# A two-layer graph kernel: the edge stage sums two blocks into the same banks, ten blocks' raw rows go ahead instead of seven, and the second aggregation gathers seven units a block

## What is computed

```python
h = relu(layernorm(x))
h1 = relu(sage_conv(h, src, dst, W1l, W1r, b1))      # mean over in-edges of h[src] @ Wl.T, + b + h @ Wr.T
x = x + sage_conv(h1, src, dst, W2l, W2r, b2)
h = relu(layernorm(x))
e = relu(concat([h[src], h[dst], edge_attr]) @ W1 + b1)
x = x + segment_mean(e @ W2 + b2, src)               # mean over the edges of each src
```

## Time and profile before

| what | us |
|---|---|
| median of 3 runs | 6354.2 (6326.7 to 6368.4) |
| the profiled execution | 6340.2 |
| its span | 6338.4 |
| PE busy | 4354.8 (69%) |
| DVE busy | 3739.4 (59%) |
| POOL busy | 2891.2 (46%) |
| ACT busy | 2546.9 (40%) |

### The profile page before, as it was taken

The page is one execution under the profiler, slowest core; times in us unless marked ns, Lnnn a source line. Parts: engine busy times, 40 slices in busy tenths (PEclk is TensorE's granted clock), DMA queues, the critical chain, the costliest instruction groups (busy, mean ns, idle before and its releaser), DMA issues. The chain is left out here.

```text
span 6338.4 us, 173060 instructions
## 1 busy us (share of the span) xinstructions
PE 4354.8 (69%) x64842; PEld 3895.0 (61%) x64842; DVE 3739.4 (59%) x6428; ACT 2546.9 (40%) x5151; POOL 2891.2 (46%) x2761
## 2 busy tenths in 40 slices
PE   3889888885777777743666666666666656666656
PEld 3778777774767666643655556556556555555656
DVE  7888888885655556553544554544544544545456
ACT  2445445443444444422433333333333333333334
POOL 2666656654554545454333443443433443444341
PEclk8999999997999989975777777777777777777778
DMA  4533233333444433323342333333333333334332
GB/s 87 124 92 76 71 74 75 74 74 95 113 113 108 107 80 85 81 56 103 97 106 89 100 103 98 99 101 99 100 93 101 103 97 107 97 94 111 92 97 60
DMA packets 509079, 591.17 MB, mean 93 GB/s; under 512 B 203666, under 2 KB 462721, under 8 KB 508278
## 3 DMA queue, kind: packets, MB, share of 16 engines
q1 hardware_dynamic: 423190, 479.51, 28.5%
q0 software_dynamic: 84032, 103.47, 6.9%
q10 hardware_dynamic: 1266, 0.31, 0.0%
HBM read 481.80 MB, written 101.17 MB: 92 GB/s over the span
## 5 line engine op out<-in xcount | busy, mean ns | idle before, releaser
L1603 POOL DMA_INDIRECT sorted_edges<-edge_rows,edge_index x1356 | 1321.7, 975 | 2015.9 <-ACT edge_rows L1725 1554.6
L1110 POOL DMA_INDIRECT conv_got<-parts_table,conv_index x1060 | 1235.4, 1165 | 876.8 <-PE conv_sums L1156 336.6
L1225 ACT CAST conv_rows<-conv_rows_ps 128x384 bf16<-128x384 f32 x2226 | 999.3, 459 | 1283.1 <-PE conv_rows_ps L1139 1040.0
L1139 PE MATMUL conv_rows_ps<-parts,conv_hot_t 128*128 128x192 bf16 x8268 | 1111.2, 256 | 451.7 <-ACT conv_rows L1225 237.0
L1689 PE MATMUL edge_sums<-edge_parts,edge_hot 128*128 128x64 bf16 (+1 forms) x15582 | 792.9, 209 | 565.5 <-issue 516.5
L1674 PE MATMUL edge_a_ps<-parts,edge_hot_t 128*128 128x64 bf16 x15582 | 792.9, 213 | 469.6 <-issue 466.2
L1156 PE MATMUL conv_sums<-conv_rows,conv_hot_d 128*128 128x193 bf16 (+1 forms) x8268 | 1103.4, 255 | 0.5 <-issue 0.4
L1689 PEld LDWEIGHTS edge_sums<-edge_parts,edge_hot 128*128 128x128 bf16 x15582 | 674.8, 108 | 668.7 <-issue 607.9
L1139 PEld LDWEIGHTS conv_rows_ps<-parts,conv_hot_t 128*128 128x128 bf16 x8268 | 698.4, 101 | 587.3 <-ACT conv_rows L1225 286.5
L1674 PEld LDWEIGHTS edge_a_ps<-parts,edge_hot_t 128*128 128x128 bf16 x15582 | 678.6, 111 | 560.8 <-issue 558.5
L1740 ACT ACTIVATE edge_parts<-edge_a_ps 128x448 bf16<-128x448 f32 x371 | 204.9, 552 | 1850.3 <-DVE edge_a_ps L1863 1413.5
(11 more groups left out here) (208 smaller groups left out, 5161.0 us busy)
## 6 DMA issues: line engine op xcount, KB each, us to landing
edge_slot_row<-slot_rows SPq DMA_DIRECT2D x371, 224.0 KB
conv_slot_row<-slot_rows SPq DMA_DIRECT2D x424, 192.0 KB
edge_edges<-sorted_edges SPq DMA_DIRECT2D x322, 224.0 KB
conv_slot_row<-slot_rows SPq DMA_DIRECT2D x318, 160.0 KB
edge_dst_row<-dst_rows SPq DMA_DIRECT2D x226, 192.0 KB
edge_attr<-in_edge_attr SPq DMA_DIRECT2D x225, 192.0 KB
sorted_edges<-edge_rows,edge_index POOLq DMA_INDIRECT x1356
sorted_edges<-conv_zero SPq DMA_DIRECT2D x28, 632.0 KB
```

The source lines that it names most:

```text
L1110: pool.indirect_dma_start(got[g][:, f, 0:PARTS * D], None, k.parts_table, bass.IndirectOffsetOnAxis(ap=index[h][:, g, at:at + 1], axis=0)) ...
L1139: mm = pe.matmul(rows_ps[(bs * h + i) % banks][:, at:at + PARTS * D], hot_t[home[g]][:, v, u * P:(u + 1) * P], k.parts[:, 2 * (GU * g + u) ...
L1225: act.copy(rows[i % bufs][:, 0:n, 0:PARTS * D], rows_ps[(bs * h + i) % banks][:, 0:n * PARTS * D].rearrange("p (u d) -> p u d", u=n)).then ...
L1603: pool.indirect_dma_start(k.sorted, bass.IndirectOffsetOnAxis(ap=index[s.part.ring][0:used, at:at + 1], axis=0), rows[j][0:used, t, :], No ...
```

## The change

Three things. (1) Ten blocks are early instead of seven. A round has six items, five of them ordinary, and there are eight rounds behind one early item and ahead of four. The ring in HBM holds five blocks, early chunks ahead of the edge stage are 46, and POOL sends four scatters a block in the second aggregation; SP loads the chunks as fast. (2) In a round the items go in pairs, and groups alternate: group g of one block, then group g of the other, then g+1. PE sums both into the same banks without a start in between (`opens`, `closes`), and DVE adds them once. Buffers turn by the place in the order (`r`), no longer by g. 25 parts are spread over the 42 slots of a round. The first round is written out, the other seven are a loop. (3) In the second aggregation one unit of each group is gathered, seven a block, and the others are expanded.

```diff
-EARLY, ROUND, ROUNDS, AHEAD, STARTED, EARLY_AT = 7, 7, 6, 3, 4, 2
+EARLY, ROUND, ROUNDS, STARTED = 10, 5, 8, 3
+LONG = (ROUND + 1) * NG
-EARLY_BUFS, BETWEEN, AFTER = 4, 5, 3
+EARLY_BUFS, BETWEEN, AFTER, EACH = 4, 5, 3, 4
...
-        fetched = [1 + g % 2 for g in range(NG)]
+        fetched = [1 + g % 2 if sorting else 1 for g in range(NG)]
...
-                    if b % 3 == 0:
-                        k.early.load(sp, BETWEEN + EARLY_BUFS + (b // 3 - 2))
+                    if b >= 3:
+                        k.early.load(sp, BETWEEN + 2 + EACH * b // ET)
...
-                    k.early.scatter(pool, 2)
+                    k.early.scatter(pool, EACH)
...
-                    pe.wait_ge(got_landed[g], 16 * fetched[g] * (done + b + 1))
+                    pe.wait_ge(got_landed[g], 16 * fetched[g] * (b + 1) + 16 * (1 + g % 2) * done)
...
         def round_group(i, s):
-            w, g = s // NG, s % NG
-            item, parity = AHEAD + (ROUND + 1) * i + w, (AHEAD + w) % 2
-            if w == EARLY_AT:
-                return Group(item, g, True, i + 1, parity, None)
-            n = AHEAD - 1 + w - (1 if w > EARLY_AT else 0)
-            return Group(item, g, False, ROUND * i + n, parity, n % RB)
+            d, s = s // LONG, s % LONG
+            pair_no, at = s // (2 * NG), s % (2 * NG)
+            g, side = at // 2, at % 2
+            early = pair_no == 1 and side == 0
+            n = (side, 2, 3 + side)[pair_no]
+            before = (at + 1, 2 * NG + g + 1, 3 * NG + at + 1)[pair_no]
+            index = i + (d + 1) if early else ROUND * i + (ROUND * d + n)
+            done = NG * i + (NG * (d + 1) + g + 1) if early else ROUND * NG * i + (ROUND * NG * d + before)
+            return Group(LONG * i + (LONG * d + s + NG), LONG // NG * i + (LONG // NG * d + s // NG + 2), s % NG, g, early, index, done,
+                         6 * i + (6 * d + 2 * pair_no + side + 1), 3 * NG * i + (3 * NG * d + NG * (pair_no + 1) + g), n, side == 0, side == 1)
 
         def round_part(i, p):
-            n, j = p // ES, p % ES
-            w = n - (AHEAD - 1)
-            read = AHEAD + (ROUND + 1) * i + w + (1 if w >= EARLY_AT else 0)
-            return Part(ROUND * i + (n + STARTED), j, (n + STARTED) % RB, read)
+            d, m, j = p // (ROUND * ES), p // ES % ROUND, p % ES
+            return Part(ROUND * i + (ROUND * d + STARTED + m), j, (STARTED + m) % RB, 6 * i + (6 * d + (1, 1, 3, 3, 5)[m]))
...
-                wait_alone(act, third_made, group.number + 1)
+                wait_alone(act, third_made, group.number + NG)
...
-                        dve.wait_ge(scattered[s], 16 * ET * Part(b - 3, s, None).times)
+                        dve.wait_ge(scattered[s], 16 * ET * Part(b - 2, s, None).times)
...
             def sum_up(group):
-                    if w % GU == 0:
-                        pe.wait_ge(added, 2 * group.number + half + 2)
+                    if w % GU == 0 and group.opens:
+                        pe.wait_ge(added, 2 * group.tally + half + 2)
...
-                        mm = pe.matmul(to[:, 0:n], hot[at][:, u, v * P:(v + 1) * P], parts[at][:, u, i, 0:n], start=(i == 0), stop=(i == PARTS - 1), skip_group_check=True)
+                        mm = pe.matmul(to[:, 0:n], hot[at][:, u, v * P:(v + 1) * P], parts[at][:, u, i, 0:n], start=(group.opens and w % GU == 0 and i == 0),
+                                       stop=(group.closes and w % GU == GU - 1 and i == PARTS - 1), skip_group_check=True)
...
-                if s.two_back is not None:
+                if s.two_back is not None and s.two_back.closes:
                     add_sums(s.two_back)
```

More of the change, by code:

```diff
@@ L1376, with __init__ @@
 class Group:
-    def __init__(self, item, g, early, index, parity, ring):
-        self.item, self.g, self.early, self.index, self.parity, self.ring = item, g, early, index, parity, ring
-        self.number = NG * item + g
-        self.done = NG * index + g + 1
+    def __init__(self, number, turn, r, g, early, index, done, item, tally, ring, opens, closes):
+        self.number, self.turn, self.r, self.g = number, turn, r, g
+        self.early, self.index, self.done, self.ring = early, index, done, ring
+        self.item, self.tally, self.opens, self.closes = item, tally, opens, closes
+        self.parity = 1 if closes else 0
 class Part:
@@ L1533, in take @@
             def take(group, before):
-                g, item = group.g, group.item
+                g, r = group.g, group.r
+                made = group.number + 1
+                if not isinstance(made, int):
+                    made = sp.to_reg(made)
                 if g == 0 and not group.early:
@@ L1540, in take @@
                         wait_positive(sp, scattered[s], both[min(s, 1)])
-                if g == 0 and group.early and not isinstance(item, int):
+                if g == 0 and group.early and not (isinstance(group.index, int) and group.index == 0):
                     for j in range(1, ES):
                         k.early.wait_chunk(sp, EARLY * ES - ES + j)
-                    sp.wait_ge(expanded, NG * (item - 3) + 2 * NG)
-                sp.wait_ge(hot_t_made, group.number + 1)
-                sp.wait_ge(other_made, group.number + 1)
-                sp.dma_start(slot_row[g][:], k.slot_rows[bass.ds(block_of(group), 1), g * GU * P:(g + 1) * GU * P].to_broadcast([P, GU * P])).then_inc(row_landed[g], 16)
-                if before is None and g >= NG - 2:
+                    sp.wait_ge(expanded, group.number + 1 - 2 * NG + NG)
+                sp.wait_ge(hot_t_made, made)
+                sp.wait_ge(other_made, made)
+                sp.dma_start(slot_row[r][:], k.slot_rows[bass.ds(block_of(group), 1), g * GU * P:(g + 1) * GU * P].to_broadcast([P, GU * P])).then_inc(row_landed[r], 16)
+                if before is None and r >= NG - 2:
                     sp.wait_ge(split, 2 * GROUPS)
@@ L1595, in slot @@
                     if s.part.read is not None:
-                        for g in range(NG):
-                            pool.wait_ge(edges_landed[g], 16 * (s.part.read + 1))
+                        for landed in edges_landed:
+                            pool.wait_ge(landed, 16 * s.part.read)
                 wait_alone(pool, rows_ready, s.part.q + 1)
@@ L1640, in early_turn @@
             def early_turn(group, part):
-                pe.wait_ge(edges_landed[group.g], 16 * (group.item + 1))
+                pe.wait_ge(edges_landed[group.r], 16 * group.turn)
                 pe.wait_ge(attr_ready, part.q + 1)
@@ L1678, in sum_up @@
             def sum_up(group):
-                at = home[group.g]
+                at = home[group.r]
                 pe.wait_ge(third_made, group.number + 1 + NG + 1)
@@ L1843, in make_hot_t @@
             def make_hot_t(group):
-                g, at = group.g, home[group.g]
-                dve.wait_ge(row_landed[g], 16 * (group.item + 1))
-                dve.wait_ge(expanded, group.number + 1 - since[g] + NG)
-                dve.tensor_scalar(hot_t[at][:, 0, :], slot_row[g][:], k.node_of[:, 0:1], None, ALU.is_equal).then_inc(hot_t_made, 1)
+                g, at = group.g, home[group.r]
+                dve.wait_ge(row_landed[group.r], 16 * group.turn)
+                dve.wait_ge(expanded, group.number + 1 - since[group.r] + NG)
+                dve.tensor_scalar(hot_t[at][:, 0, :], slot_row[group.r][:], k.node_of[:, 0:1], None, ALU.is_equal).then_inc(hot_t_made, 1)
             def make_early_hot(group):
@@ L1887, in add_sums @@
                     dve.wait_ge(summed, 2 * (group.number + NG) + half + 1)
-                    dve.wait_ge(added, 2 * group.number + half + 2)
+                    dve.wait_ge(added, 2 * group.tally + half + 2)
                     dve.tensor_tensor(part, part, sums[half][:, 0:GU * D1].rearrange("p (w d) -> p w d", d=D1), ALU.add).then_inc(added, 1)
```

85 lines of the change are left out of this document (42 added, 43 removed).

## The result

On the same chip, in turns with the kernel before, the changed kernel takes 6107.6 us (median of four, 6089.8 to 6110.1) and the kernel before 6344.8 us (6326.7 to 6368.4): a ratio of **0.962, interval 0.959 to 0.965**, 237 us less. Forecast were 6262 us, with a range from 6140. The sign is right; the size is 2.8 times the forecast's 85 us, and the time lies under the range.

A forecast was written before the change was run, and what follows sets the result against it. Runs of indirect scatters were taken to stop PE in the edge stage. Terms -89 - 21 - 13 + 35 + 3 = -85 took 6340.2 to 6255 us; 6262 was named, between that and 6269, range 6140 to 6370.

The forecast's parts named there:

- The second aggregation, +35 forecast: Second aggregation: two more scatters and three fewer gathers a block, with added matmuls, cost +0.78 us a block, +35 us in all.
- the gather's price of 0.6 us: Second aggregation: each gather taken away saves 0.6 us, chosen between 0.50 and 0.71.
- The bound of -9 for this stage: Second aggregation, lower bound: every POOL DMA at one price, 0.59 us, gives -0.09 us a block, -9 in all.
- P at a = 4.39: Edge stage: P, a part's PE work and six scatters, put at 7.22 us if an ordinary group (a) takes 4.39.
- Parts and early blocks -89: Edge stage: 15 fewer parts (90 scatters) and 21 groups turned early save 89 us, the middle of -68 and -110.
- adds -21: Edge stage: pairing two blocks relieves 182 groups of DVE's adds, saving 21 us, bounds 0 and -195.
- Projection ahead -13 forecast: Projection ahead of the edge stage: POOL sends 28 early scatters instead of 38, saving 13 us, bounds 0 and -16.
- First aggregation +3 forecast: First aggregation: three more early blocks are cleared at 1.1 us each, costing 3 us.
- Rival 1, VectorE's turn decides: Edge stage body: DVE's turn bounds it, so saved adds count: 6102 us in full, 6200 at half; chance 0.20.
- Rival 2, the toll only moves: Scatters cost the same in aggregation and edge stage, gathers were cheap, adds hidden: 6337 us, no change; chance 0.22.
- Rival 3, slower by runs of scatters: Second aggregation: four scatters make a run of five, removed gathers cost nothing: +153 us there, 6415 in all; chance 0.11.
- Rival 4: The change doesn't do what it says: paired order costs a wait each round or parts bunch; 6290 to 6300 us.

## Why the prediction was wrong, point by point

- **The second aggregation, +35 forecast, -114 found, is the step that failed, and in it the gather's price of 0.6 us.** It came from dividing ten gathers' 5.0 us by ten or by seven, as if each cost alike. By runs: three gathers fewer a block, and nothing else, gave 1208.2 - 979.6 = 229 us, 1.4 us for each of the 159, though six matmuls a block were added; by the one block without scatters the seven that remain cost 1.3 us in all. What has a price is the place in a run, and not the gather: without the second gathers the runs are shorter, and 122 DMAs fewer stand third or later. The trace before had shown the stop in a run of scatters. The prediction used it for its slower rival alone, and not for gathers taken away. It also read it as "every further one", where the second still leaves PE 23 matmuls in 1.28 us and only from the third on it stands nearly still.
- The scatter's price was right: 1.04 us forecast. Seven gathers alone against the change, the same but for two scatters more in fifty blocks (and a little else), are 979.6 and 1093.7: 1.14 us each, though across two sets of runs.
- The bound of -9 for this stage was no bound. It spread the difference of two kinds of block evenly over their DMAs, which is one more even price, and it divided by 12 although the short block has three DMAs itself: by 9 it is 0.79 us each and about -20 in all. That too is far from -114. (P at a = 4.39 comes to 7.20 and not 7.22, on which nothing rests.)
- Parts and early blocks -89, adds -21: together -110 forecast, -133 found. The split is not settled in the slow condition. Where no scatter runs, groups of the change alternate 3.3 and 4.4 us where all took 4.4, as the earlier trace rows led to expect.
- Projection ahead -13 forecast, -10 found. First aggregation +3 forecast; all that stands ahead of the second came to -5: too small to tell.
- Not foreseen: the last projection's clock, +29 in this execution. It can come without the change, as said above.
- *Rival 1, VectorE's turn decides*: its 6102 us are within 6 us of the median, for another reason, which is luck. In the slow condition PE waited 0.4 us for the adds in the changed body and 19.1 before; nearly half of the gain came in the aggregation, where that rival kept the forecast's +35. In the quick condition, which no trace of before showed, VectorE's turn does bound the groups, and the adds are worth 91 us of the 195 at which the rival priced them.
- *Rival 2, the toll only moves*: its first half is right. A scatter costs 1.14 us in the aggregation, and in the edge stage (3163.5 - 1695.5)/1266 = 1.16 us, slow condition less quick. The Trainium skill, "DMA: Bandwidth & Descriptors", Specifications, says that transfers under 512 B miss line rate. The two prices here are alike; but the same rows cost PE nothing in the quick condition or 2.21 us apart, so what they measure is PE's stop, not their transfer. Its second half, cheap gathers, failed as the forecast did.
- *Rival 3, slower by runs of scatters*: the four do form a run, and the two more of a block cost 2 x 1.14 = 2.3 us, near the 2.56 that it gave them. But the three gathers that it priced at nothing gave 4.3.
- *Rival 4*: no new wait shows, neither at a round's end nor on SP. GpSimd's wait for the ring's blocks to be loaded is 62.1 us in eight waits, and was 75.0 in eight.

So in the slow condition seven gathers in place of ten are worth as much alone as with the rest (0.961; 0.962 and 0.958 for the change, each in its own set of runs). The rest gives about as much in the edge stage as its scatters cost in the aggregation. In the quick condition the same change is worth 0.981, by other bounds.

No kernel was found that is the fastest in both conditions. The change with one clearing behind each scatter is the fastest in the slow one (5514 us); in the quick one it was not run, and by an estimate from its spacing GpSimd's 2013 us would stand there against the edge stage's 1695.

## What to carry to other kernels

Before dividing a stage's loss by its instructions, ask whether each costs the same where it stands. Here an indirect DMA alone on GpSimd cost next to nothing, the second of a run little in the aggregation, and from the third on PE nearly stood still; a row that showed the stop was already in hand. Price an edit by the runs that it shortens or lengthens, and count them in the timeline, not in the source: a wait ahead of them can join the gathers of several groups. And where the bounds of two parts follow each other closely, undo a part of the finished change as well as adding it alone: in the quick condition seven gathers gave nothing alone, and the change gave nothing without them.

## What the runs showed that was not expected

- One kernel takes 4280 or 6250 to 6350 us, a factor of up to 1.48, and by whole sets of runs: of eight sets (the first result among them) four were slow and four quick, on one chip both. What sets the condition no profile shows, and it was not tried.
- In the slow condition indirect DMAs of a run that start 1.3 us apart nearly stop PE's issue from the third on (2 to 3 matmuls a us in the edge stage, while ACT and DVE do little either), and 1.59 us apart they slow it; in the quick one 27 a us run beside them. By what path is open.
- In the slow condition, slowing GpSimd down by 0.3 us a scatter made the kernel faster: a ratio of 0.869 against the 0.958 to 0.962 of the change.
- PE stayed at 0.50 of full clock, 1.2 GHz, through the whole last projection (61.6 us busy of 69) in all three traces of the changed kernel and in one of two of the kernel before; in the other it went at 0.92, which is worth 26 to 29 us. Kernels with the same code there show both, so 0.6% of a time in the quick condition can be this alone.
